# Layer 0 of a four-layer graph network: the inverse softmax sums travel by DMA through DRAM, row blocks are weighed in pairs, and half of the next scores goes ahead of the value sums

## The reference

```python
def _L0_gnn_ref(x, adj_matrix, Wq, bq, Wk, bk, Wv, bv, Wo, bo, gamma, beta):
    CHUNK = 128; NUM_HEADS = 4; EPS = 1e-05
    q, k, v = ...                      # (B, H, N, Dh): 8, 4, 1024, 32
    kc = k.reshape(B, H, Nc, CHUNK, Dh)
    vc = v.reshape(B, H, Nc, CHUNK, Dh)
    scores = jnp.einsum('bhnd,bhjcd->bhnjc', q, kc) / jnp.sqrt(Dh)
    scores = jnp.clip(scores, -10.0, 10.0)
    scores = jnp.where(mask == 0, -10.0, scores)
    attn = jax.nn.softmax(scores, axis=-1)       # one softmax per block of 128 keys
    ctx = jnp.einsum('bhnjc,bhjcd->bhnd', attn, vc)
    out = ctx @ Wo.T + bo + x
    ...                                # layernorm over F, gamma, beta
    return out
```

## Time and profile before

| | us |
|---|---|
| median of 3 runs | 2156.48 (2144.48 to 2159.27) |
| the profiled execution | 2157.34 |
| its span, first to last instruction | 2155.5 |
| layer 0, first exponential to the last reciprocal | 56.75 to 753.23 |
| TensorE busy (matmuls) in the span | 1736.7 (81%) |
| VectorE busy | 1595.2 (74%) |
| ScalarE busy | 1346.2 (62%) |
| mean granted TensorE clock | 0.902 |

### The profile page before, as it was taken

The page is one execution under the profiler, slowest core; times in us unless marked ns, Lnnn a source line. Parts: engine busy times, 40 slices in busy tenths (PEclk is TensorE's granted clock), DMA queues, the critical chain, the costliest instruction groups (busy, mean ns, idle before and its releaser), DMA issues. The chain is left out here.

```text
span 2155.5 us, 37200 instructions
## 1 busy us (share of the span) xinstructions
PE 1736.7 (81%) x13876; PEld 1102.1 (51%) x13876; DVE 1595.2 (74%) x2790; ACT 1346.2 (62%) x1767; POOL 111.6 (5%) x130
## 2 busy tenths in 40 slices
PE   2888888888888827699899977797877776999997
PEld 1344343443344325577677755675656553555554
DVE  2676767677767746678888889988988965767674
ACT  2665645555455517577677778988889834545553
POOL 0000000101000010000000000000000000000000
PEclk9999989999899957899999988998988988999999
DMA  6413031130311021111111112221112202000000
GB/s 191 98 40 79 1 79 40 41 79 1 79 40 40 1 82 55 35 40 50 41 40 41 50 51 70 70 70 61 61 60 70 79 26 79 11 10 20 10 10 20
DMA packets 50270, 108.92 MB, mean 51 GB/s; under 512 B 7633, under 2 KB 26450, under 8 KB 50098
## 3 DMA queue, kind: packets, MB, share of 16 engines
q1 hardware_dynamic: 50098, 106.54, 17.1%
HBM read 68.37 MB, written 4.59 MB: 34 GB/s over the span
## 5 line engine op out<-in xcount | busy, mean ns | idle before, releaser
L1052 ACT ACTIVATE g<-s_all,steep_d 128x1024 fp8e4<-128x1024 f32 x608 | 642.3, 1135 | 42.1 <-DMA s_all<-s_rows 26.4
L993 PE MATMUL acc<-parts,g 128*128 128x102 bf16 (+1 forms) x6144 | 418.0, 229 | 28.5 <-DVE sums L1143 19.3
L993 PEld LDWEIGHTS acc<-parts,g 128*128 128x128 fp8e4 x6144 | 401.6, 99 | 61.6 <-issue 43.8
L975 PE MATMUL post<-parts,edge 128*128 128x396 bf16 (+1 forms) x1024 | 232.9, 383 | 83.7 <-DVE base L1151 83.7
L558 ACT ACTIVATE e<-s_ps 128x1024 f32<-128x1024 f32 x256 | 248.9, 1022 | 37.0 <-PE s_ps L390 26.6
L1136 DVE TENSOR_TENSOR g<-g,edge 128x1024 int32<-128x1024 int32 x192 | 227.7, 1218 | 34.6 <-ACT g L1052 34.6
L564 ACT ACTIVATE chunk<-ctx_ps 128x512 f32<-128x512 f32 x128 | 76.2, 596 | 243.1 <-PE ctx_ps L420 243.1
L386 PE MATMUL s_ps<-qs,ks 128*128 128x512 f32 x512 | 207.4, 517 | 12.4 <-issue 7.5
L975 PEld LDWEIGHTS post<-parts,edge 128*128 128x128 fp8e4 x1024 | 102.2, 102 | 191.3 <-issue 106.6
L704 DVE SCALAR_TENSOR_TENSOR e<-e,bound 128x1024 f32<-128x1024 f32 x160 | 189.8, 1220 | 8.4 <-ACT e L558 8.4
L420 PE MATMUL ctx_ps<-e,v 128*32 128x512 f32 x1024 | 152.7, 668 | 48.8 <-DVE weighed L725 42.0
(11 more groups left out here) (157 smaller groups left out, 2208.8 us busy)
## 6 DMA issues: line engine op xcount, KB each, us to landing
s_all<-s_rows SPq DMA_DIRECT2D x96, 512.0 KB, 3.6
qs<-split SPq DMA_DIRECT2D x128, 128.0 KB, 2.3
ks<-split SPq DMA_DIRECT2D x128, 128.0 KB, 2.3
x<-in_x SPq DMA_DIRECT2D x8, 512.0 KB, 6.0
adj_in<-in_adj SPq DMA_DIRECT2D x8, 512.0 KB, 4.1
out_x<-x SPq DMA_DIRECT2D x8, 512.0 KB, 3.2
parts<-in_adj_t SPq DMA_DIRECT2D x6, 512.0 KB, 6.0
chunk<-in_adj_t SPq DMA_DIRECT2D x4, 512.0 KB, 6.5
```

Of the source, the lines that this page charges most:

```text
L975: ins = pe.matmul(self.post[:, it % 2, 0:H * 3 * W1].rearrange("p (h k c) -> p h k c", h=H, k=3), self.c.edge[:, jt, it * P:(it + 1) * P], ...
L993: ins = pe.matmul(self.acc[:, bank, o:o + self.NS], self.g[:, h % RING, jt, it * P:(it + 1) * P], self.upper[par][:, jt, h, :, :].rearrang ...
L1052: act.activation(self.g[:, h % RING, jt, :], self.s_all[:, h % 2, :], ACT.Relu, bias=self.steep_d[par][:, jt, h:h + 1], scale=STEEP, satur ...
```

## The change

The inverse sums are no longer spread by TensorE. `invert` is one reciprocal into `inv`. SyncE stores it by 8 DMAs (8 rows of 256 values each) into a DRAM tensor, waits for them, and loads the blocks two at a time into `inv_all` by 4 DMAs for a pair (one for each head, 32 rows each, 1024 contiguous values read for every row); `inv_all` has two slots. So a stage has 16 stores and 32 loads beside the 32 DMAs of `stack`. On SyncE's list, the stores, the wait for them and the loads of pairs 0 and 1 of half 0 stand ahead of `stack` of q, the load of pair 2 stands between the stacks of q and k, and that of pair 3 behind them; the stores and loads of half 1 stand at the head of the next stage.

`weigh` runs at even steps: one multiplication of 128 x 1024 on SBUF operands, and for pairs 1 to 3 one addition of 128 x 1024. Half 0 is weighed at steps 10, 12, 14 and 0, half 1 at 2, 4, 6 and 8. `values` waits only for `copy_chunk` of the step before; `copy_chunk` waits until the pair that lay in its place has been weighed. On TensorE one of the two `scores` of a step goes ahead of `values`; on ScalarE the first exponentials of a step go ahead of `copy_chunk`. The 0/1 matrices, their three loads and the 16 activations that made them are gone.

```diff
+        inv_dram = nc.dram_tensor("inv_rows", (2, H, T, HALF), F32, kind="Internal").ap()
+            def store_inverses(b, half):
+                m = 2 * b + half
+                wait_apart(c, sp, inverted, m + 1)
+                for h in range(H):
+                    for q in range(2):
+                        sp.dma_start(inv_dram[half, h, :, q * QUARTER:(q + 1) * QUARTER],
+                                     inv[h * DH + q * T:h * DH + (q + 1) * T, :]).then_inc(inv_stored, 16)
+                wait_apart(c, sp, inv_stored, 128 * m + 128)
+            def load_inverses(b, half, pairs):
+                m = 2 * b + half
+                for p in pairs:
+                    wait_apart(c, sp, pair_weighed, 4 * m + p + 3)
+                    for h in range(H):
+                        sp.dma_start(inv_all[h * DH:(h + 1) * DH, p % 2, :, :].rearrange("d j n -> d (j n)"),
+                                     inv_dram[half, h, 2 * p:2 * p + 2, :].rearrange("j n -> (j n)").partition_broadcast(
+                                         DH)).then_inc(inv_loaded[p % 2], 16)
             def stage(b, par, first, more):
                 if first:
-                    sp.wait_ge(selected, 16)
                     ...
+                else:
+                    store_inverses(b - 1, 1)
+                    load_inverses(b - 1, 1, range(4))
+                store_inverses(b, 0)
+                load_inverses(b, 0, (0, 1))
                 if more:
-                    prepare(b + 1, 1 - par)
+                    wait_apart(c, sp, s_ready, 32 * b + 64)
+                    stack_q(b + 1, 1 - par)
+                load_inverses(b, 0, (2,))
+                if more:
+                    stack_k(b + 1, 1 - par)
+                load_inverses(b, 0, (3,))
...
             def values(b, par, i):
                 pe.wait_ge(chunk_copied, 16 * b + i + 1)
-                pe.wait_ge(chunk_weighed, 16 * b + i + 1)
...
-                    if not (first and i < 9):
-                        pe.wait_ge(chunk_copied, 16 * b + i)
-                        spread_inverses(b, i)
                     if not (first and i == 0):
                         sums(before[0], before[2])
-                        values(*before)
                     if more or i + 1 < STEPS:
                         if i + 1 == STEPS:
                             stacks(n)
-                        for hp in range(2):
-                            scores(*after, hp)
+                        scores(*after, 0)
+                    if not (first and i == 0):
+                        values(*before)
+                    if more or i + 1 < STEPS:
+                        scores(*after, 1)
...
-                act.wait_ge(late_loaded, 128)
-                for x in range(16):
-                    act.activation(spread[:, x // 8, x % 8, :], same_head, ACT.Copy,
-                                   scale=row_is[:, x:x + 1]).then_inc(selected, 1)
...
             def copy_chunk(b, i):
                 act.wait_ge(pv_done, 16 * b + i + 3)
-                act.wait_ge(chunk_weighed, 16 * b + i + 1)
+                act.wait_ge(pair_weighed, 8 * b + i // 2 + 1)
                 act.activation(chunk[:, i % T, :], ctx_ps[:, :], ACT.Copy).then_inc(chunk_copied, 1)
             def stage(b, par, first, more):
                 for i in range(STEPS):
+                    exps(b, i, 0)
                     if i >= 2:
                         copy_chunk(b, i - 2)
                     elif not first:
                         copy_chunk(b - 1, i + STEPS - 2)
-                    exps(b, i, 0)
                     exps(b, i, 1)
...
             def invert(b, half):
                 ...
-                dve.reciprocal(inv, sum_ps).then_inc(sums_read, 1)
-                dve.wait_ge(sums_read, m + 2)
-                dve.tensor_copy(inv_hi, inv).then_inc(inv_cut, 1)
-                ...
+                    dve.wait_ge(inv_stored, 128 * m)
+                dve.reciprocal(inv[:, :], sum_ps).then_inc(inverted, 1)
             def weigh(b, i):
-                ...
+                half, p = pair_at(i)
+                m = 2 * b + half - (0 if i >= 10 else 2)
+                dve.wait_ge(inv_loaded[p % 2], 64 * (2 * m + p // 2 + 1))
+                dve.wait_ge(chunk_copied, 8 * m + 2 * p + 3)
+                if p > 1:
+                    dve.wait_ge(added, 2 * m + p - 1)
+                acc = ctx_sb[:, half, :, :]
+                dve.tensor_tensor(weighed[:, :, :] if p else acc, chunk[:, 2 * p:2 * p + 2, :], inv_all[:, p % 2, :, :],
+                                  ALU.mult).then_inc(pair_weighed, 1)
+                if p:
+                    dve.wait_ge(pair_weighed, 4 * m + p + 5)
+                    dve.tensor_tensor(acc, acc, weighed[:, :, :], ALU.add).then_inc(added if p < 3 else ctx_ready, 1)
```

More of the change, by code:

```diff
@@ L199, in layer0 @@
         pick = sb("pick", [P, 48])
-        spread = sb("spread", [P, 2, T, P], F32R)
-        minus_low = sb("minus_low", [P, 1])
+        inv_all = sb("inv_all", [P, 2, 2, HALF])
         wq, wk, wv, wo = (sb(k, [P, F]) for k in ("wq", "wk", "wv", "wo"))
@@ L254, in layer0, with pair_at @@
         block = ctx.enter_context(nc.Block())
-        def weighed_at(i):
-            return int(1 <= i <= 8), (i - 1) % T
+        def pair_at(i):
+            return int(2 <= i <= 8), (i - 2) % T // 2
         @block.sync
@@ L303, in stage, with tail @@
                         sp.dma_start(const3[k:k + 1, :], const_parts[:, k, :]).then_inc(const_stored, 16)
-                if more:
-                    prepare(b + 1, 1 - par)
-            walk(sp, prepare, stage)
+                else:
[3 more added lines that the diff above has]
+                load_inverses(b, 0, (0, 1))
+                if more:
+                    wait_apart(c, sp, s_ready, 32 * b + 64)
[4 more added lines that the diff above has]
+                load_inverses(b, 0, (3,))
+            def tail():
+                store_inverses(B - 1, 1)
+                load_inverses(B - 1, 1, range(4))
+            walk(sp, prepare, stage, tail)
         @block.gpsimd
@@ L396, in sums @@
                 pe.wait_ge(p_ready, 32 * b + 2 * i + 2)
-                if jt == 0:
-                    pe.wait_ge(sums_read, 2 * b + half + 1)
+                if jt == 0 and not (isinstance(b, int) and b == 0 and half == 0):
+                    pe.wait_ge(inverted, 2 * b + half)
                 for q in range(2):
@@ L484, in tail @@
                 sums(B - 1, STEPS - 1)
-                pe.wait_ge(chunk_copied, 16 * B)
-                spread_inverses(B, 0)
                 values(B - 1, 1, STEPS - 1)
-                for i in range(1, 9):
-                    if i == 1:
-                        pe.wait_ge(chunk_copied, 16 * B + 1)
-                    else:
-                        pe.wait_ge(chunk_weighed, 16 * B + i - 1)
-                    spread_inverses(B, i)
-                    if i == 2:
-                        output(B - 1, 0)
+                output(B - 1, 0)
                 output(B - 1, 1)
@@ L771, in stage @@
                 for i in range(STEPS):
-                    if not (first and i < 9):
+                    if first and i == 10:
+                        dve.wait_ge(const_stored, 48)
+                    if i % 2 == 0 and not (first and i < 10):
                         weigh(b, i)
@@ L775, in stage @@
                     if i == 8:
-                        if first:
-                            dve.wait_ge(const_stored, 48)
                         invert(b, 0)
@@ L801, in tail @@
             def tail():
-                for i in range(9):
-                    weigh(B, i)
-                    if i == 0:
-                        invert(B - 1, 1)
-                        update(B - 2, 1)
-                    elif i == 3:
-                        residual(B - 1, 1, 0, False)
-                    elif i == 6:
-                        update(B - 1, 0)
+                weigh(B, 0)
+                invert(B - 1, 1)
+                update(B - 2, 1)
+                residual(B - 1, 1, 0, False)
+                weigh(B, 2)
+                weigh(B, 4)
+                update(B - 1, 0)
+                weigh(B, 6)
+                weigh(B, 8)
                 residual(B - 1, 1, 1, False)
```

53 lines of the change are left out of this document (15 added, 38 removed).

## The result

| | before | after |
|---|---|---|
| median, us | 2155.65 (11 runs, 2144.48 to 2159.27) | 2164.89 (11 runs, 2155.18 to 2174.53) |
| the profiled execution, us | 2157.34 | 2162.02 (span 2160.2) |
| ratio of the medians | | 1.0045 [1.0025, 1.0065] |
| mean granted TensorE clock | 0.902 | 0.900 |
| first exponential to the last reciprocal of layer 0 | 56.75 to 753.23 | 52.91 to 764.77 |

What follows compares the result with a forecast made beforehand. Layer 0 was taken as bound by a ring through `values`, copy, spread and weighing, then a DMA chain. Terms +43 - 23 - 17 + 2 - 4.5 - 1 came to 0: 2157 us, range 2098 to 2202.

Steps and rivals of the forecast that it cites:

- A: Start of the reciprocal of step 8 to `high` of k: 23.85 us against 17.7, +6.2 x 7 stages = +43.
- C: Reciprocal of step 0 to that of step 8: 41.75 us against 45.0, -3.2 x 7 = -23.
- B: `high` of k to the reciprocal of step 0: mean 24.1 us against 26.6, -2.5 x 7 = -17.
- parts 3 and 4: Inverse chain, reciprocal to weighing, 11.35 us, no worse than before; SyncE's stores and loads delay `stack` of q, +43.
- rival of the cheap SyncE: SyncE's issues cost the low end, A is 21.4 us: 2133 us in all; chance 0.08.
- rival "slower": SyncE's queue bounds reciprocal of step 8 to `high` of k, stores costing what stacks do: 2194 us; chance 0.26.
- the loosened ring: Bank passing from `values` to copy, spread, weighing and back; the change loosens it, priced only within C and B.
- rival "faster": `e` and the freed TensorE absorb idle times in C and B, VectorE runs through: 2103 us; chance 0.24.
- part 7: TensorE's half-clock spells, one more made sure by the stall in A: 3 us a stage in C and B.
- parts 8 and 9: Last stage 38.9 us, +2.3; exponentials can start at 52.2, -4.5; tail 24 us, -1.
- part 9: Early first score and early first exponentials cost nothing and are already in the hand-made order.
- `stack` of k hidden: It lands some 15 us after `high` of k; the next stage's first scores are due at about 17.

Runs made afterwards that it cites:

- e2: Changed kernel with the load of pair 1 of half 0 moved behind the stack of q on SyncE: 2147.47 us, 0.9972 of before.
- e3: Changed kernel with the inverses of a half stored by one DMA in place of 8, loads reading two runs a row: 2148.31 us, 0.9971 of before.
- r5: Changed kernel with pair 1 loaded behind the stack of q, one store a half, and residual of half 1 one step later: 2120.28 us, 0.9837 of before.
- r9: Changed kernel with a split buffer of its own for k, part of the mask left out (result not the reference's): 2106.5 us, 0.9788 of before.
- e4: Changed kernel with VectorE's residual of half 1 moved from step 14 to 15: 2155.41 us, 1.0006 of before.
- r8: Changed kernel with eight small zero products on TensorE while `high` of k waits: 2160.61 us, 4.3 faster than the changed kernel.
- e6: Changed kernel with ScalarE's order put back, `copy_chunk` ahead of the first exponentials: 2220.2 us, 1.0292 of before.
- r11: As r10, with `low` of k, the values' projection and its copy each one step later: 2135.51 us.
- r10: On r5: `high` of k waits only for the 8 DMAs of q that read the high half, `low` of k for the others: 2124.93 us.
- e1: Changed kernel with all stores and loads of the inverses issued by GpSimd, stacks left on SyncE: 2195.4 us, 1.018 of before.

## Why the prediction was right, and where it wasn't

"As before" was right within 1%, and the time is 7.9 us from the forecast, inside its own range. Of the mechanism the loss in A is there, as is the gain in C. But of the two terms that were to pay for A one came (C) and one did not (B). That the sum still came near 0 is in part luck: B missed by 21 us to the slow side, A by 9 and C by 2.5 to the fast side.

1. *Chain and A (parts 3 and 4).* Right in kind: SyncE's order is what costs. Forecast 23.85, measured 22.78; +34 for +43 (+41.6 against the mean of 17.91; the 43 was taken against stage 4 alone). The term mis-sized is the spacing of the stores: 0.55 taken, 0.33 measured (8 in 2.63), so that the low bound, from the one isolated store, was the true one. The last store starts 2.3 instead of 3.9 us after the first, 1.6 us less a stage. The rest of stage 4 is close: the first load follows the last store's start by 1.6 us (1.8 taken), the eight loads take 3.85 (3.8) and the stack 12.95 (12.6). For the weighing, pair 0 landed 3.0 us after its fourth load (that load starts at about 461.5, the weighing at 464.51) where 2.5 was taken. e2, e3 and r5 show that the queue is the cause: each issue taken away ahead of the stack comes back in A. r9 shows how much hangs on the wait altogether, some 52 us. The rival of the cheap SyncE had its stores right and its loads (0.37) wrong, hence a loss in A between the two.

2. *The queue as the bound with stores at 0.67 (rival "slower")* is out: it was to decide from 10.5 us between the reciprocal's end and the stack, and there are 7.8.

3. *C (part 5).* Right: 41.34 for 41.75. The first weighing comes 10.7 us after the reciprocal, for 11.35. In the rest of C of stage 4 VectorE is busy 26.0 us and idle 4.9, where 25.5 and 3.9 with 1 for the clock were laid out; of the idle time 1.7 is at step 5, as forecast. But this isn't the loosened ring alone: with TensorE's order put back (e5) C is 44.22, only 0.8 less than before, and this order alone in the kernel before (r12) gives 42.68. The two together make the 3.6 us. The rival "faster" with C at 37.9 is out; the ring is still there in another form, as the copy's waits for the pairs (69.0 and 51.8 us) show.

4. *B (part 6).* This is the step that failed: 24.1 forecast, 27.12 measured, 3.0 us a stage or 21 us. The working's terms, against the means of stages 1 to 6 (24.8 forecast, 27.8 measured), read from VectorE's instructions in B: busy 19.2 us for 18.4; until `high` is done 1.15 for 1.2; until the output product 3.5 for 2.3; waits for exponentials 3.2, where 0.9 and 2 for the clock were taken; the other 0.7 are small gaps and one idle of 2.25 us ahead of a weighing in stage 3. So two terms were too small. The output product: before it was waited for 2.1 us a stage, and the working took that over; moved out of the way (e4) it gave back 1.2 us. The busy time: three pairs, six blocks, are weighed in B where five were, and one addition of stage 4 took 1.65 us; the working took the 18.4 over as they were. Stage 0 has no output product in B and still took 23.2 us for the 20 forecast; VectorE waits 5.0 us for exponentials there. Why the output product comes later than before, and stage 0's waits, are open.

5. *The clock (part 7).* A spell at half clock stands behind the stall, as forecast: 0.87 against 0.94 in B of stage 4. Its price was not too low: the 3.8 us more at the lower level (7.0 for 3.2) are 1.9 us less work, and the products of r8, which take B back to 0.94, win 1.05 us where 2 had been put in. Whether the 1 us of C was right no run tells, since r8 left C as it was.

6. *Last stage, start, tail (parts 8 and 9).* +1.7 for +2.3. The exponentials start at 52.91, not 52.2: a table load of 1.28 us stands directly ahead of the first of them in both profiles (55.46 before, 51.61 after), and the working left it out. The first scores start 0.75 us earlier than before (50.35), which makes up for part of it. -2.6 for -1 in the tail.

7. *The orders (part 9).* They "cost nothing", and that is true; but the text gave them no price in the other direction. Without TensorE's the same change would be 1.5% slower than before (e5), without ScalarE's 2.9% (e6), instead of 0.45%: C as forecast contains them. Most of what TensorE's order is worth in the time comes only with the change (1.0% against 0.2% in r12).

8. *`stack` of k hidden*, "by 2 us only": held, except for 2.9 us in all in r9 and 2.8 in r11.

## What to carry to other kernels

When a DMA chain is put on an engine's list, count the issues that then stand ahead of every other transfer on it, and put only those in front whose reader comes first: one moved pair of loads was worth as much here as one store for eight. When a serial resource is taken out of a ring, look for the wait that is next in each list (here a buffer shared by q and k, some 52 us) and reorder the lists by which wait is due last; TensorE's order, worth 0.2% in the time before, was worth 1.0% after, and ScalarE's 2.5%. And a wait moved off one engine (r10, r11, e1) counts only if the engine that inherits it has slack.

## What the runs showed of the hardware

SyncE's issues are not alike. Stores of 8 rows of 1 KB from SBUF to DRAM come every 0.33 us back to back, loads of 32 rows of 4 KB every 0.45, the same rows as two runs of 2 KB every 0.56 (8 in 4.51), and copies of 32 rows of 4 KB between SBUFs every 0.63 to 0.67 (16 in 10.07 here, in 10.74 before). On GpSimd a store takes 0.57 (8 in 4.52) and the first load starts 2.77 us behind the last issue, against 1.3 on SyncE; from the fourth load's issue to the weighing it is about 5 us, against 3. One store of 128 rows of 1 KB is followed by its dependent load after 1.97 us, hardly more than the 1.84 of the small `s_rows` store. And eight products of 15 columns by 256 in a stall of 7 us kept the granted clock of the stretch behind it at 0.94 instead of 0.87 (stage 4; the means of seven stages are 0.94 and 0.86).
